# Gated Flamingo block: norms spread by 32-row tiles, sums for eight units at a time, values made beside the norms

## The reference

```python
def attn_layer(x, Wqkv, qs, ksc, Wo):          # 16 heads of 64 channels
    q, k, v = split(x @ Wqkv)                  # x with half its channels shifted by a token
    q = l2norm(q) * qs;  k = l2norm(k) * ksc
    q = q * cos * scale + rotate_half(q) * sin * scale
    k = k * cos / scale + rotate_half(k) * sin / scale
    out = local_attention(q, k, v)             # windows of 32, each sees itself and the one before
    return out @ Wo
def ffn_layer(x, g, bln, W1, b1, W2, b2):
    a, gate = split(norm(x) @ W1 + b1)         # 341 hidden channels each
    return a * gelu(gate) @ W2 + b2
for i in range(6):
    x = attn_layer(shift_tokens(x), ...) + x
    x = ffn_layer(shift_tokens(x), ...) + x
```

## Time and profile before

| | before |
|---|---|
| median of three runs | 2108.72 us |
| the profiled execution, and its span | 2106.88 us, 2105.1 us |
| mean granted TensorE clock | 0.965 |
| TensorE matmuls busy | 1920.0 us, 91% |
| VectorE busy | 1564.3 us, 74% |
| ScalarE busy | 1073.1 us, 51% |
| GpSimd busy | 899.1 us, 43% |
| matmuls in the program | 35408 |

### The profile page before, as it was taken

One profiled execution on the slowest core, in us unless ns is written; L12 is line 12 of the kernel. 1 busy time (PEld: TensorE's weight loads), 2 busy tenths in 40 slices (PEclk: granted clock), 3 DMA queues, 4 the chain that ended last, 5 costly groups with the idle time before them and its releaser, 6 DMA issues.

```text
span 2105.1 us, 84728 instructions
## 1 busy us (share of the span) xinstructions
PE 1920.0 (91%) x35408; PEld 1292.9 (61%) x35408; DVE 1564.3 (74%) x3092; ACT 1073.1 (51%) x1879; POOL 899.1 (43%) x1231
## 2 busy tenths in 40 slices
PE   6888866799999999999999999999999999999996
PEld 3444423566666666666676667666666766676664
DVE  4555546678787887878787878788887878787873
ACT  2333332446555555556464656555555656464553
POOL 1000004445455554545453645445554545454541
PEclk9888877999999999999999999999999999999997
DMA  1000104555566555656465665556665646554551
GB/s 65 6 10 20 40 0 69 75 79 86 78 116 107 85 87 85 105 99 100 80 89 83 111 104 86 80 81 107 105 98 81 90 78 117 102 85 74 87 81 39
DMA packets 73332, 166.87 MB, mean 79 GB/s; under 512 B 16592, under 2 KB 23504, under 8 KB 72400
## 3 DMA queue, kind: packets, MB, share of 16 engines
q0 software_dynamic: 36864, 100.71, 35.7%
q1 hardware_dynamic: 36432, 65.68, 12.7%
HBM read 20.57 MB, written 1.05 MB: 10 GB/s over the span
## 4 chain that ended last, share of the span: by engine, by line
PE 55%; DVE 16%; DMA 13%; issue 10%; POOL 3%; ACT 2%; DVEq 0%; POOLq 0%; SPq 0%; ACTq 0%
PE ps L1002 13%; DMA big<-big 13%; PE ps L1037 9%; PE ps L1013 5%; PE ps L1074 4%; PE ps L1061 4%; PE ps L935 4%; PE ps L1091 4%; DVE big L807 3%; POOL big L477 3%; DVE big L804 3%; PE ps L915 2%; DVE big L838 2%; DVE big L825 2%; PE ps L1104 2%
## 5 line engine op out<-in xcount | busy, mean ns | idle before, releaser
L477 POOL DMA_DIRECT2D big<-big x768 | 606.1, 1490 | 68.3 <-DVE big L807 57.9
L1002 PE MATMUL ps<-big,wn_sb 128*128 128x256 f32 x1536 | 395.0, 393 | 24.3 <-issue 14.9
L564 ACT ACTIVATE big<-ps 128x512 f32<-128x512 f32 x384 | 229.0, 597 | 336.7 <-PE ps L1002 330.4
L1002 PEld LDWEIGHTS ps<-big,wn_sb 128*128 128x128 f32 x1536 | 274.0, 191 | 102.1 <-issue 46.5
L815 DVE TENSOR_TENSOR big<-big,ps 128x512 f32<-128x512 f32 x384 | 243.5, 681 | 101.3 <-PE ps L1025 50.1
L577 ACT ACTIVATE big<-ps 128x512 f32<-128x512 f32 x192 | 114.7, 597 | 367.8 <-PE ps L1037 367.8
L820 DVE TENSOR_REDUCE top<-ps 128x8 f32<-128x512 f32 x192 | 123.3, 684 | 205.9 <-PE ps L1061 205.9
L804 DVE TENSOR_TENSOR big<-ps,tab 128x512 f32<-128x512 f32 x384 | 258.1, 682 | 9.3 <-ACT big L564 9.3
L807 DVE TENSOR_TENSOR big<-ps,tab 128x512 f32<-128x512 f32 x384 | 257.9, 682 | 0.0
L468 POOL TENSOR_TENSOR big<-big 128x512 f32<-128x512 f32 x96 | 121.7, 1267 | 299.7 <-ACT big L581 299.7
L1145 PE MATMUL ps<-big,wo_sb 128*128 128x256 f32 x768 | 214.1, 382 | 0.1
(11 more groups left out here) (146 smaller groups left out, 3009.5 us busy)
## 6 DMA issues: line engine op xcount, KB each, us to landing
big<-big POOLq DMA_DIRECT2D x768, 128.0 KB, 4.9
big<-big SPq DMA_DIRECT2D x96, 256.0 KB, 3.5
big<-big SPq DMA_DIRECT2D x96, 192.0 KB, 3.7
wn_sb<-in_wn SPq DMA_DIRECT2D x6, 1024.0 KB, 9.0
wn_sb<-in_wn SPq DMA_DIRECT2D x6, 512.0 KB, 4.8
wo_sb<-in_wo SPq DMA_DIRECT2D x6, 512.0 KB, 3.3
w_sb<-in_w SPq DMA_DIRECT2D x6, 341.0 KB, 2.9
w_sb<-in_w SPq DMA_DIRECT2D x6, 192.0 KB, 2.9
```

What stands on the lines that cost most here:

```text
L477: eng.dma_start(rot[to:to + 32, at:at + 4, :], src[32 * r:32 * r + 32], accum_op=ALU.add).then_inc(added[i], 16)
L564: eng.activation(sq[:, two, :], ps[:, i % 2, :].rearrange("p (a t) -> p a t", a=2), ACT.Square).then_inc(sq_d, 1)
L1002: mm = eng.matmul(ps[:, k % 2, a * T:a * T + T], wn_sb[:, u * P:u * P + P], sT, start=True, stop=True)
```

## The change

Four things change.

The selection by tiles: the lengths of unit `u` now stand in 32-row group `QUAD[u]`, at place `SLOT[u]` there. A matmul of `spread` reads only the 32 rows of that group. One step R does two pairs, into both banks, going from one pair to the other; their two units stand in different row groups. So there are `R0 R2 R4 R6` for eight steps.

The sums: `g1` and `g3` do eight units each in two rounds of four, in place of four steps `g0` to `g3`.

The values: `V0` waits for the rotation steps to have read bank 0, and no longer for H6 and H7. The first spread waits for the eviction of the last values, and `k0` and `k1` wait for H6 and H7.

The orders of TensorE, ScalarE and VectorE are written anew. GpSimd's stays.

```diff
+QUAD = [u // 2 % 2 + 2 * (u // PAIRS) for u in range(UNITS)]
+SLOT = [u % 2 + 2 * (u // 4 % 2) for u in range(UNITS)]
...
-            rsel[32 * (u % 4) + 8 * c + 2 * (u // 4) + p // D, u, p] = 256
+            rsel[32 * QUAD[u] + 8 * c + 2 * SLOT[u] + p // D, u, p] = 256
...
-            S0 k0 k1 F1 S1 k2 k3 T0 g0 T1 F2 k4 k5 W0 W1 g1 g2 k6 T2 k7 U0 T3 g3 W2 W3 U1 F4 O0 O1 O2 U2 O3 U3
-            F5 R0 R1 O4 R2 O5 R3 O6 R4 F6 R5 R6 O7 F7 R7 V0 V1 V2 V3""".split()]
+            S0 k0 k1 F1 S1 k2 k3 T0 T1 F2 k4 k5 g1 W0 W1 T2 k6 T3 k7 U0 U1 g3 W2 W3 V0 V1 V2 V3 F4 R0 O0 U2 U3
+            O1 R2 F5 O2 O3 R4 O4 O5 F6 O6 R6 O7 F7""".split()]
         ACT_PLAN = [(x_[0], int(x_[1:])) for x_ in """
-            s0 s1 x0 F1 s2 s3 t0 F2 t1 s4 s5 x1 s6 t2 s7 u0 t3 F3 n0 u1 F4 u2 u3 F5 v0 v1 v2 v3""".split()]
+            s0 s1 x0 F1 s2 s3 F2 t0 t1 x1 s4 s5 s6 t2 t3 s7 u0 n0 v0 v1 F3 v2 u1 v3 F4 u2 u3 F5""".split()]
         DVE_PLAN = [(x_[0], int(x_[1:])) for x_ in """
-            X0 X1 D0 D1 c0 c1 d0 d1 X2 X3 D2 c2 d2 c3 d3 D3 Z0 f0 c4 d4 c5 d5 f1 Y0 f2 c6 f3 Z1 n0 d6 c7 Y1 N1
-            d7 N2 N3 N4 N5 N6 H0 H1 H2 F5 H3 H4 F6 H5 H6 H7 F7 e0""".split()]
+            X0 X1 D0 D1 c0 c1 d0 d1 X2 X3 c2 d2 c3 d3 D2 D3 f0 Z0 f1 c4 d4 c5 d5 Y0 f2 c6 d6 f3 n0 c7 d7 Z1 N1
+            N2 N3 N4 N5 N6 Y1 H0 H1 H2 H3 F5 H4 H5 F6 H6 e0 H7 F7""".split()]
...
                         if i >= 4:
-                            eng.wait_ge(sums, it * 4 + (i // 2 - 1))
+                            eng.wait_ge(sums, it * 4 + 2)
...
-                        if Bh:
-                            eng.wait_ge(vev, it * 4)
+                    if k < 2 and Bh:
+                        eng.wait_ge(hat_d, it * PAIRS + (k - 1))
...
                 def head_sums(g):
+
                     eng.wait_ge(sq_d, it * PAIRS + (2 * g + 2))
-                    if g == 0 and Bh:
+                    if g == 1 and Bh:
                         eng.wait_ge(ss_d, it)
                         eng.wait_ge(x_d, it - 1 + FREE)
...
+                    for a in range(2):
+                        for n in range(4 * g - 4 + a, 4 * g + 4, 2):
+                            u = ORDER[n]
+                            q = QUAD[u]
+                            mm = eng.matmul(ps[32 * q:32 * q + 32, 2, 0:T], sumsel[:, SLOT[u], :], sq[:, n % 8, :],
+                                            start=g == 1 and a == 0, stop=g == 3 and a == 1, skip_group_check=True)
+                        mm.then_inc(sums, 1)
 
                 def spread(n):
+
                     if n == 0:
                         eng.wait_ge(r_d, it + 1)
-                    if n < 2:
-                        eng.wait_ge(rot_d, it * PAIRS + (7 + n))
+                        eng.wait_ge(vev, it * 4 + 4)
                     else:
-                        eng.wait_ge(hat_d, it * PAIRS + (n - 1))
+                        eng.wait_ge(hat_d, it * PAIRS + n)
+                    eng.sem_inc(r_go, 1)
                     for a in range(2):
-                        mm = eng.matmul(ps[:, n % 2, a * T:a * T + T], rselb[:, 2 * HATS[n] + a, :], n_parts, start=True, stop=True)
-                    mm.then_inc(rb, 1)
+                        for m in (n, n + 1):
+                            u = 2 * HATS[m] + a
+                            q = QUAD[u]
+                            mm = eng.matmul(ps[:, m % 2, a * T:a * T + T], rselb[32 * q:32 * q + 32, u, :], n_parts[32 * q:32 * q + 32, :],
+                                            start=True, stop=True, skip_group_check=True)
+                            if a == 1:
+                                mm.then_inc(rb, 1)
 
                 def values(j):
...
                     if j < 2:
-                        eng.wait_ge(hat_d, it * PAIRS + (7 + j))
+                        eng.wait_ge(rot_d, it * PAIRS + (7 + j))
```

More of the change, by code:

```diff
@@ L239, in gated_flamingo @@
                              "wo_d", "x_d", "w_go", "s_go", "vf_free", "y2_d", "den_h", "den_s"))
-        chain, nchain, nmid = sem("chain"), sem("nchain"), sem("nmid")
+        chain, nchain, nmid, r_go = sem("chain"), sem("nchain"), sem("nmid"), sem("r_go")
         nmean, nxc, nsq, nvar, nva, nln, ny, nxn, nt = (
```

## The result

| | before | after |
|---|---|---|
| median | 2107.56 us (4 runs) | 2058.03 us (4 runs, 2055.98 to 2063.42) |
| ratio to before, 95% interval | | 0.9774 [0.9755, 0.9792] |
| span of the profiled execution | 2105.1 us | 2054.2 us |

Forecast were 2059 us and a range of 2020 to 2104.

The account below looks back on a forecast made before the run. TensorE's own list of work, with small holes, was taken to bound the pass; 0.45 plus 0.53 for DMAs made 1.0 us a pass, 46 for 46 passes, plus 4 in the first: 50 off, 2059 us; range 2020 to 2104.

Parts of the forecast that it names:

- the middle: From k4 to U0: worth nothing, the front's 0.7 us given back behind F2; bounds -0.5 and +1.0.
- Part 1, the values: V moves between W3 and F4: still 3.63 us of work, but now covering VectorE's chain of norms.
- The hole of 0.5 at R0: TensorE waits at R0 for ScalarE's last value eviction, from 25.0 to 25.5 us; bounds nil to 1.4.
- Part 2, the tiles: Four R steps over 32-row tiles replace eight: 0.43 us each, 1.8 in all; ends 1.0 and 2.6.
- That is what the eight cost: The four tiled R steps take 1.8 us, against 1.76 for the eight steps before.
- R steps of 0.43 to 0.50: Sign of the forecast in TensorE's timeline: tiled R steps beside O take 0.43 to 0.50 us.
- Rival B: No price for the tiles' change of shape: four R steps 1.0 us, 37 us more gained, 2022; chance 0.20.
- Part 3: Sums for eight units: g's of 0.57, 1.00 and 0.57 us become two of 1.00, saving 0.14 a pass.
- The list from U0: TensorE's steps from U0 to the next S0 take 17.8 us, with the new hole; before, 18.35.
- The wait goes: H steps' DMA wait vanishes: m3 lands at 28.5 us, H5 not before 31; mean pass gains 0.53 us more.
- rival D: SyncE's value copies collide with m3, landing at 32.6 us; net 0.4 us lost a pass, 2123; chance 0.15.
- 4 had been laid for V: In the first pass V fills TensorE's 4.98 us wait for the norms before R0, saving 4 us.

Follow-up runs that it names:

- e7: Kernel before with V0 to V3 behind W3, their evictions behind n0, and d7 ahead of Y1 and N1; 2085.29 us, ratio 0.9886.
- e8: e7 with full-shape spreads two at a time, other steps between, and VectorE's H steps reordered to match; 2062.05 us, ratio 0.9792 to the kernel before.
- e1: Changed kernel with each spread matmul over all 128 rows again, steps, order and waits kept; 2058.62 us, ratio 0.9764 to the kernel before.
- e5: Changed kernel with V0 to V3 back behind F7 and their evictions behind F5; 2212.17 us, ratio 1.0494 to the kernel before.
- e4: Changed kernel with each spread step's four tiled matmuls issued twice in a row; 2109.85 us, ratio 0.9995 to the kernel before.
- e3: Changed kernel with SyncE's four copies of the values waiting until m3's DMAs have landed; 2048.22 us, ratio 0.9704 to the kernel before.
- e9: e8 with SyncE's copies of the values waiting for m3's DMAs; 2029.11 us, ratio 0.9606 to the kernel before.

## Why the prediction was right

The total was 2059 and is 2058, in part by errors that cancel. The span fell by 50.9 us. The first F2 comes 12.5 us earlier (407.15 before, 394.67 after), where 4 were laid; the 46 passes give 37.3, where 46 were laid; the end gives 1.1, where nothing was. That 8.5 too much ahead of the stretch meets 9 too little in it is luck. What was right is the kind of the gain and its main parts: it comes from TensorE's list in the quiet pass, the norms are covered by V, and the middle gives nothing. A quiet pass gained more than laid, the DMAs less: between the two laid-out passes it is 35.22 to 34.55, 0.67 for the forecast 0.45, and of the 0.53 for the DMAs 0.14 is left in the mean.

The runs split the usual pass: 35.75 before, 35.11 with the values early and d7 ahead (e7), 34.11 with the spreads two by two (e8), 34.32 with the new first half and the sums for eight (e1), 34.53 with the tiles (the change). For e8 this is the commonest pass, without the waits for DMAs. So the first two steps shorten the quiet pass and the last two lengthen it.

*Part 1, the values (right in its cover, its hole mis-sized).* The norms are covered by V: R0 has no wait for them, and e5 shows the 2.34 us that stand open without V, 1.30 of them for the norms themselves. The hole of 0.5 at R0 is hardly there. F4 to R0 is 1.06 us with tiles and 1.03 with full-shape spreads, where F4 alone takes 0.87. The term was too large because ScalarE's steps were laid end to end at 0.60. In a row they follow each other by less, as this timeline of ScalarE after shows (v1, F3, v2, u1, v3):

```profile
1250.65 0.60 ACT L582 ACTIVATE big<-ps 128x512 f32<-128x512 f32 x1 [0.26 <-PE ps L1050]
1251.15 0.59 ACT L604 ACTIVATE big<-big,vf 128x256 f32<-128x256 f32 x1
1251.64 0.59 ACT L582 ACTIVATE big<-ps 128x512 f32<-128x512 f32 x1
1252.11 0.60 ACT L592 ACTIVATE big<-ps 128x512 f32<-128x512 f32 x1
1252.59 0.61 ACT L582 ACTIVATE big<-ps 128x512 f32<-128x512 f32 x1
```

The starts are 0.47 to 0.50 apart. The row of two s steps at 1234.76, 1.18 for two of 0.60, said nearly nothing of it. The timeline of before had other neighbours that did, an s step at 1238.92 and a t step at 1239.42 among them, and they should have been read.

*Part 2, the tiles (right, a little too kind).* "That is what the eight cost" is nearly confirmed by e1; they cost 0.21 a pass more, where 0.04 had been laid. The sign that was named, R steps of 0.43 to 0.50, was not seen: a tiled R takes 0.32 to the next start, and the other 0.15 lies in the steps on its two sides. Rival B, the gain without a price for the change of shape, is out: the 0.11 a step is there, but is paid back. e4 shows that inside one shape the saving is whole. The rule of the Trainium skill that was weighed here (TensorEngine Tiling (Array Packing), Key Properties: changing the mode drains the engine) agrees with the run, at 0.15 us a stretch. The prediction's 1.0 us for four R steps is the price with two row groups beside each other, not what the page's factor of four would give (1.76 / 4 = 0.44).

*Part 3 and the middle (right).* k6 at 14.5 and U0 at 16.9 are as laid, and g1 and g3 take 1.00 each. The bounds of -0.5 and +1.0 were not needed.

*The end of the pass.* The list from U0 was laid with 17.8 and is 17.6. But the text had the gain down to 0.45 a pass, from holes not named. e7 and e8 name them: with spreads one at a time TensorE waited for the H steps, and with the new order of the pass's end, which takes them two by two, the best pass is 1.0 us shorter. That is the largest part of the gain in a quiet pass, and the prediction had only written "small holes".

*The DMAs (the step that failed).* "The wait goes" is wrong. It fell from 47.6 us to 21.1. The issue was laid rightly, with its end at 24.4. The landing was laid 4.1 us later, at 28.5, as in a pass where nothing else moves, and H5 at 31 or later. In the median pass m3 lands 5.3 us after its last issue, at 29.8, and H5 starts at 30.6, so the margin is 0.8 us and not 2.5. The copies were held for a rival with 0.15. The collision of rival D is real, and the waiting copies of e3 and e9 show its price: 10 us in the changed kernel, 33 in e8. It is not large enough to make the change slower, because in the usual pass m3 lands just before H5 needs it, though the copies run beside it from 24.96 on. It shows where GpSimd issues late (12.5 us of the waits, in three passes) and where SyncE loads weights (8.3, in four others), which the sum had left out as unchanged; no run held the weights back, so their part is argued and not shown. Each long wait can also cost clock, as in the pass above. So the mean pass gained 0.81 us and not 1.0: 37 for 46.

*The first passes.* Of the 12.5 us ahead of the first F2, 6.0 lie before the first pass, in code that is not changed. Here is the first k step, before and after:

```profile
320.60 3.68 PE L1002 MATMUL ps<-big,wn_sb 128*128 128x256 f32 x8 [14.95 <-issue]
```

```profile
314.64 3.67 PE L1007 MATMUL ps<-big,wn_sb 128*128 128x256 f32 x8 [14.95 <-issue]
```

These 6 us are a difference between two executions, not a gain of the change: in the eleven profiled executions the first k step starts at 314.6 to 322.7, and the six with the changed kernel's front (314.6, 317.5, 322.7, 322.3, 316.1, 321.4) lie on both sides of before's 320.6. The remaining 6.5 lie in passes that the change touches. The first pass, from its first k step to the first S0, is 2.7 us shorter (33.0 to 30.3), where 4 had been laid for V in the place of the wait of 4.98; after the change TensorE waits there 1.45 us before each of R2, R4 and R6. The second pass gives 2.9, which the sum didn't count. How much of this is the change's is open, since e1, whose edit hardly touches these passes, spent 5.7 us more in them. By the profiled executions, without the 6 us the span would have fallen by 45 and not by 50, well inside the range.

## What to carry to other kernels

Two steps that share a bank tie two engines' orders together. When one is moved, look for every step that still holds the bank: here d7 alone turned a gain of 1% into a loss of 2%. Where each step of one engine waits for a small step of another, as R does for H here, try them in pairs with other work between (e8). And a transfer that is made ready earlier starts earlier, into whatever is then in flight; if nobody needs it soon, let it wait for the one that is needed (e3, e9).

## What the runs showed of the hardware

- bf16 matmuls over 32 rows in two row groups, going to two banks by turns, take 0.055 us each (0.22 for four, e4), full-shape ones 0.11.
- A stretch of four such matmuls between full-shape fp32 ones lengthens the steps on its two sides by about 0.09 and 0.06 us, which is more than the 0.11 it saves (changed kernel and e1).
- ScalarE's evictions of 128x512 fp32 show 0.60 us each, but can start 0.47 to 0.50 after the step before.
- The last of m3's accumulating DMAs of 128 KB landed 4.6 us after their issue with no copies near (before), 5.2 with the copies held back (e9), and 6.3 with four copies of 192 and 256 KB begun 0.9 us ahead of the end of the issue (e8); all are medians.
- GpSimd had idle times at its DMA issues for which no wait is named: 24.6 us in 46 gaps in the changed kernel, 40 of about 0.24 and six of up to 3.0, and 10.4 in 4 before, of up to 3.7. Their cause stays open.
- With two holes of 1.04 and 1.30 us in each pass (e5) TensorE was granted 1.2 GHz for a part of 17 of 46 passes, at 1.4 to 2.7 us each.
- The same first stage took 314.6 to 322.7 us in eleven executions.
